# Four opening stages of a graph network kernel become one block

## The reference

```python
x_heads = jnp.einsum('ni,hij->nhj', x, W)          # node table: x @ W0
src = x_heads[row]; dst = x_heads[col]             # rows gathered by edge
edge_gate = jax.nn.sigmoid(edge_attr @ eg_w.T + eg_b)
e = einsum('ehd,hd->eh', src, a_src) + einsum('ehd,hd->eh', dst, a_dst) + edge_bias
```

## Time and profile before

| | |
|---|---|
| runs | 9183.11, 9192.17, 9197.33 us |
| median | 9192.17 us |
| span of the profiled execution | 9188.8 us (its own time outside the span is not recorded) |
| share of the span busy | PE 71%, DVE 69%, POOL 69%, ACT 18% |
| instructions | 193747 |

### The profile page before, as it was taken

One profiled execution on the slowest core, in us unless ns is written; L12 is line 12 of the kernel. 1 busy time (PEld: TensorE's weight loads), 2 busy tenths in 40 slices (PEclk: granted clock), 3 DMA queues, 4 the chain that ended last, 5 costly groups with the idle time before them and its releaser, 6 DMA issues. The chain is left out here.

```text
span 9188.8 us, 193747 instructions
## 1 busy us (share of the span) xinstructions
PE 6564.0 (71%) x41828; PEld 5489.2 (60%) x41829; DVE 6345.2 (69%) x11929; ACT 1632.9 (18%) x4649; POOL 6369.9 (69%) x7772
## 2 busy tenths in 40 slices
PE   5999999999378548777777625999768850037752
PEld 3878877888267536666666524777558740026652
DVE  3444444444577868777777524888768899999965
ACT  1111111110221134444444200111410000011100
POOL 2777777775068557777777764888367778877774
PEclk9999999999789879999999857999889975569975
DMA  3777777777067436666666769999359963359974
GB/s 115 207 206 208 208 207 206 209 207 200 24 177 210 128 113 211 209 208 209 209 209 208 213 172 157 273 270 270 103 163 264 259 188 86 87 159 256 253 210 115
DMA packets 2113959, 1742.97 MB, mean 190 GB/s; under 512 B 376688, under 2 KB 1838118, under 8 KB 2113686
## 3 DMA queue, kind: packets, MB, share of 16 engines
q1 hardware_dynamic: 1217548, 819.30, 30.4%
q10 hardware_dynamic: 710140, 472.87, 20.6%
q0 software_dynamic: 186160, 449.72, 17.3%
HBM read 1289.62 MB, written 453.29 MB: 190 GB/s over the span
## 5 line engine op out<-in xcount | busy, mean ns | idle before, releaser
L1592 POOL DMA_INDIRECT z_xg<-table,srci x1664 | 1819.1, 1093 | 512.9 <-issue 466.3
L1162 POOL DMA_INDIRECT sorted<-m_rows,srci x1612 | 1609.0, 998 | 532.4 <-issue 436.1
L464 POOL DMA_INDIRECT g_xg<-table,srci x1612 | 1582.1, 981 | 491.2 <-issue 464.3
L1458 PE MATMUL n_ps<-n_row,n_oh 128*128 128x257 f32 x3712 | 881.2, 389 | 216.0 <-DVE n_row L1434 198.1
L483 PE MATMUL g_psg<-g_wg,g_eT 128*128 128x136 f32 x3224 | 1027.6, 474 | 0.0
L1458 PEld LDWEIGHTS n_ps<-n_row,n_oh 128*128 128x128 f32 x3712 | 677.6, 190 | 419.5 <-issue 337.4
L500 PE MATMUL g_psx<-scores,g_hot 128*128 x3608 | 835.5, 362 | 70.3 <-DVE e_score L591 68.0
L483 PEld LDWEIGHTS g_psg<-g_wg,g_eT 128*128 128x128 f32 x3224 | 769.3, 324 | 191.0 <-issue 191.0
L500 PEld LDWEIGHTS g_psx<-scores,g_hot 128*128 128x128 f32 x3608 | 806.8, 329 | 86.9 <-issue 85.9
L1656 PE MATMUL z_ps<-z_wrow,z_oh 128*128 128x132 f32 x3712 | 603.4, 315 | 329.8 <-issue 188.8
L564 DVE TENSOR_TENSOR g_y<-g_gate,g_xg 128x512 f32<-128x512 f32 x403 | 279.7, 694 | 787.5 <-DMA g_xg<-table,srci 786.8
(11 more groups left out here) (411 smaller groups left out, 12549.7 us busy)
## 6 DMA issues: line engine op xcount, KB each, us to landing
n_row<-sorted SPq DMA_DIRECT2D x464, 520.0 KB, 4.4
z_buf<-gathered ACTq DMA_DIRECT2D x464, 256.0 KB
g_keys<-dst_row ACTq DMA_DIRECT2D x451, 256.0 KB
ag_buf<-gated SPq DMA_DIRECT2D x451, 256.0 KB, 3.2
m_keys<-dst_row ACTq DMA_DIRECT2D x451, 256.0 KB
gathered<-z_xg SPq DMA_DIRECT2D x416, 256.0 KB
gated<-g_y SPq DMA_DIRECT2D x403, 256.0 KB
g_eT<-in_attr_t SPq DMA_DIRECT2D x402, 256.0 KB
```

The lines of the kernel that those rows point to most:

```text
L464: nc.gpsimd.indirect_dma_start(out=xg[:, u, j, :], out_offset=None, in_=v.table[:, :], in_offset=bass.IndirectOffsetOnAxis(ap=v.srci[:, t: ...
L1162: nc.gpsimd.indirect_dma_start(out=v.sorted[:, :], out_offset=bass.IndirectOffsetOnAxis(ap=place[:, t:t + 1], axis=0), in_=rows[:, u, j, : ...
L1458: last = nc.tensor.matmul(ps[u % 4][:, 0:ROW], oh[:, u, j, :], row[:, u, j, 0:ROW], start=(j == 0), stop=(j == G - 1))
L1592: nc.gpsimd.indirect_dma_start(out=xg[:, u, j, :], out_offset=None, in_=v.table[:, :], in_offset=bass.IndirectOffsetOnAxis(ap=v.dsti[:, t: ...
```

## The change

One block, `stage_prologue`, takes the place of `stage_constants`, `stage_weights`, `stage_node_table` and `stage_steps` for the edges. In it:

- X is the first thing that SP loads, without a wait; its last part is cut into 96 and 10 nodes; `src_row` is gone; `dst_row` and the blanks come after the index tiles. Each group of loads has a semaphore of its own. `padrow` and `blank` are set by POOL.
- ACT loads the first layer's weights at once, with 8 DMAs of 32 words for its vectors where there were 16 of 16 words; the 14 loads of the other two layers' weights are issued by ACT after the first turn of the node table.
- The table is made in 25 pairs of blocks. PE transposes straight from X, ACT copies 256 columns, PE makes two products into one bank, and ACT copies 2 x 136 columns to `row` and 2 x 8 to `scores`. DVE has no part in it. The code is written out, with no loop. SP stores a pair at a time, 136 KB.
- DVE's chain for the steps runs beside it, and PE makes the two sums after pair 11.

`stage_clear` is gone: the gate stage sets only the last 52 x 8 words of each partition of `e_score`, on DVE ahead of its first wait. `stage_steps` keeps only what its other call needs (not shown). `v.after` and the DRAM tensor `src_row` are gone.

```diff
--- before.py
+++ after.py
@@ -59,98 +59,203 @@
-def stage_constants(nc, v):
...
+def stage_prologue(nc, v, steps, follows):
+    PAIRS, R = NBX // 2, 4
...
+            @block.sync
+            def _(sp):
+                sp.dma_start(v.X[:, 0:NB - 1, :], v.x[0:full, :].rearrange("(b p) c -> p b c", p=P)).then_inc(s_x, 16)
+                sp.wait_ge(s_set, 4)
+                sp.dma_start(v.X[0:cut, NB - 1, :], v.x[full:full + cut, :]).then_inc(s_x, 16)
+                sp.dma_start(v.X[cut:TAIL, NB - 1, :], v.x[full + cut:N, :]).then_inc(s_x, 16)
+                sp.dma_start(v.srci[:, 0:TE - 1], v.src_t).then_inc(s_src, 16)
+                sp.dma_start(v.srci[0:ETAIL, TE - 1:TE], v.src[(TE - 1) * P:E, None]).then_inc(s_src, 16)
+                sp.dma_start(dsti[:, 0:TE - 1], v.dst_t).then_inc(s_blk, 16)
+                sp.dma_start(dsti[0:ETAIL, TE - 1:TE], v.dst[(TE - 1) * P:E, None]).then_inc(s_blk, 16)
+                sp.wait_ge(s_pad, 2)
+                sp.dma_start(v.dst_row[:, 1:1 + E], v.dst[None, :]).then_inc(v.s_in, 16)
+                for place in (E + 1, E + 1 + half):
+                    sp.dma_start(v.dst_row[:, place:place + half], padrow[:, :]).then_inc(v.s_in, 16)
+                for line in (v.dst_row, v.sorted_row):
+                    sp.dma_start(line[:, 0:1], blank[:, 0:1]).then_inc(v.s_in, 16)
+                    sp.dma_start(line[:, TR * P + 1:TR * P + 2], blank[:, 0:1]).then_inc(v.s_in, 16)
+                for n in range(PAIRS):
+                    sp.wait_ge(s_row, n + 1)
+                    sp.dma_start(table[:, 2 * n:2 * n + 2, :], row[:, n % R, :, :]).then_inc(s_st[n % R], 16)
+                for u in range(R):
+                    sp.wait_ge(s_st[u], 16 * ((PAIRS - u + R - 1) // R))
+                sp.wait_ge(v.s_in, 16 * 7)
...
+                pe.wait_ge(s_w0, 16 * (2 + len(first.vectors)))
+                nc.tensor.matmul(ps_w[:, 0:2 * X8], first.wt[:, :], first.ab[:, :], start=True, stop=True).then_inc(s_ab, 1)
+                pe.wait_ge(s_x, 48)
+                pe.wait_ge(s_cp, 8)
+                def turn(n):
+                    if n >= 2:
+                        pe.wait_ge(s_xt, n - 1)
+                    for j in range(2):
+                        last = nc.tensor.transpose(ps_t[n % 2][:, j * P:(j + 1) * P], v.X[:, 2 * n + j, :], v.ident[:, :])
+                    last.then_inc(s_tr, 1)
+                def rows(n):
+                    if n == 0:
+                        pe.wait_ge(s_rhs, 1)
+                    if n >= 3:
+                        pe.wait_ge(s_row, n - 2)
+                        pe.wait_ge(s_sc, n - 2)
+                    pe.wait_ge(s_xt, n + 1)
+                    for j in range(2):
+                        last = nc.tensor.matmul(ps_r[n % 3][:, j * (W + X8):(j + 1) * (W + X8)], xt[:, n % 2, j * P:(j + 1) * P],
+                                                first.rhs[:, :], start=True, stop=True)
+                    last.then_inc(s_h, 1)
+                for n in range(PAIRS + 1):
+                    if n < PAIRS:
+                        turn(n)
+                    if n >= 1:
+                        rows(n - 1)
+                    if n == PAIRS // 2:
+                        pe.wait_ge(s_dve, 8)
+                        for d in range(2):
+                            last = nc.tensor.matmul(ps_s[d][:, :], v.ones[0:NBX, 0:P], started[0:NBX, d, :], start=True,
+                                                    stop=True)
+                        last.then_inc(s_pe, 1)
+                pe.wait_ge(v.s_w, 16 * sum(2 + len(w.vectors) for w in others))
+                for n, w in enumerate(others):
+                    nc.tensor.matmul(ps_w[:, (n + 1) * 2 * X8:(n + 2) * 2 * X8], w.wt[:, :], w.ab[:, :], start=True,
+                                     stop=True).then_inc(s_ab, 1)
+            @block.scalar
+            def _(act):
+                act.wait_ge(s_set, 1)
+                weight_loads(act, first, s_w0)
+                act.dma_start(first_i[0:NBX, :], v.dst_first.broadcast_to([NBX, GE])).then_inc(v.s_first, 16)
+                nc.scalar.preload_act_table(ACT.Copy)
+                def copy(n):
+                    if n >= 2:
+                        act.wait_ge(s_h, n - 1)
+                    act.wait_ge(s_tr, n + 1)
+                    nc.scalar.activation(xt[:, n % 2, :], ps_t[n % 2][:, 0:2 * P], ACT.Copy).then_inc(s_xt, 1)
+                def rows(n):
+                    if n >= R:
+                        act.wait_ge(s_st[n % R], 16 * (n // R))
+                    act.wait_ge(s_h, n + 1)
+                    made = ps_r[n % 3][:, 0:2 * (W + X8)].rearrange("p (t w) -> p t w", t=2)
+                    nc.scalar.activation(row[:, n % R, :, :], made[:, :, 0:W], ACT.Copy).then_inc(s_row, 1)
+                    nc.scalar.activation(v.scores[:, 2 * n:2 * n + 2, :], made[:, :, W:W + X8], ACT.Copy).then_inc(s_sc, 1)
+                for n in range(PAIRS + 1):
+                    if n < PAIRS:
+                        copy(n)
+                    if n >= 1:
+                        rows(n - 1)
+                    if n == 1:
+                        act.wait_ge(s_set, 6)
+                        for w in others:
+                            weight_loads(act, w, v.s_w)
...
+                nc.vector.memset(first.ab[:, :], 0.0).then_inc(s_set, 1)
+                nc.vector.memset(v.X[:, NB - 1:NBX, :], 0.0).then_inc(s_set, 1)
+                nc.vector.memset(v.srci[:, TE - 1:TR], PADKEY).then_inc(s_set, 1)
+                nc.vector.memset(dsti[:, TE - 1:TR], PADKEY).then_inc(s_set, 1)
+                for w in others:
+                    nc.vector.memset(w.ab[:, :], 0.0).then_inc(s_set, 1)
+                nc.vector.memset(v.ones[:, :], 1.0).then_inc(s_cp, 1)
+                nc.vector.memset(v.zeros[:, :], 0.0).then_inc(s_cp, 1)
...
+                dve.wait_ge(s_ab, 1)
+                nc.vector.tensor_copy(first.rhs[:, C:C + 2 * X8], ps_w[:, 0:2 * X8]).then_inc(s_rhs, 1)
+                link = chain(dve, s_dve)
+                dve.wait_ge(v.s_first, 16)
...
+                dve.wait_ge(s_src, 32)
+                nc.vector.tensor_copy(v.srck, v.srci[:, :]).then_inc(s_keys, 1)
+                dve.wait_ge(s_blk, 32)
+                nc.vector.tensor_copy(v.dstk, dsti[:, :]).then_inc(s_keys, 1)
+                dve.wait_ge(s_pe, 1)
...
+def weight_loads(queue, w, landed):
+    queue.dma_start(w.wt[:, :], w.wt_dram).then_inc(landed, 16)
+    queue.dma_start(w.rhs[:, 0:C], w.w_dram).then_inc(landed, 16)
+    for row, first, n, col in w.vectors:
+        queue.dma_start(w.ab[first:first + n, col], row, allow_slow_non_contiguous=True).then_inc(landed, 16)
...
-def stage_node_table(nc, v, name, rhs, table, scores, loads=(), kept=W):
...
@@ -529,6 +520,7 @@
             def _(dve):
+                nc.vector.memset(e_score[:, TE:TR, :], 0.0).then_inc(s_end, 1)
                 dve.wait_ge(s_w, 16 * (2 + 2 * H))
@@ -592,7 +584,7 @@
-                dve.wait_ge(s_end, 1)
+                dve.wait_ge(s_end, 2)
                 nc.vector.tensor_copy(hist[:, :], psc[:, 0:NBX]).then_inc(s_end, 1)
...
@@ -993,14 +985,6 @@
-def stage_clear(nc, v, name, x):
-    s = v.sem(name)
-    with nc.Block() as block:
-        @block.vector
-        def _(dve):
-            nc.vector.memset(x[:, :, :], 0.0).then_inc(s, 1)
@@ -2231,9 +2215,9 @@
-                ([(v.a0[h, 16 * s:16 * s + 16, :], 16 * h, 16, X8 * s + h) for h in range(8) for s in range(2)],
-                 [(v.a1[C:2 * C, :], 0, C, 0), (v.a1[0:C, :], 0, C, X8)],
-                 [(v.a3[h, 32 * (1 - s):32 * (1 - s) + 32, :], 32 * h, 32, 4 * s + h) for h in range(4) for s in range(2)]))):
+                ([(v.a0[h].rearrange("(s p) o -> p (s o)", s=2), 16 * h, 16, slice(h, None, X8)) for h in range(8)],
+                 [(v.a1[C:2 * C, :], 0, C, slice(0, 1)), (v.a1[0:C, :], 0, C, slice(X8, X8 + 1))],
+                 [(v.a3[h, 32 * (1 - s):32 * (1 - s) + 32, :], 32 * h, 32, slice(4 * s + h, 4 * s + h + 1)) for h in range(4) for s in range(2)]))):
...
-        v.src_row = dram("src_row", (1, TR * P), I32)
...
-            stage_constants(nc, v)
-        stage_weights(nc, v)
-        stage_node_table(nc, v, "t0", v.tables[0].rhs, v.table, v.scores)
-        stage_steps(nc, v, "se", None, GE, steps_e, follows)
+        stage_prologue(nc, v, steps_e, follows)
         start.close()
         with ExitStack() as layer:
             e_score = sb("e_score", [P, TR, X8], F32, layer)
-            stage_clear(nc, v, "ce", e_score)
             stage_gate(nc, v, e_score, gated, hist, steps_e)
```

More of the change, by code:

```diff
@@ L142, in _ @@
             @block.tensor
             def _(pe):
-                pe.wait_ge(v.s_w, 16 * sum(2 + len(w.vectors) for w in v.tables))
-                for n, w in enumerate(v.tables):
-                    last = nc.tensor.matmul(ps[:, n * 2 * X8:(n + 1) * 2 * X8], w.wt[:, :], w.ab[:, :], start=True, stop=True)
-                last.then_inc(s_p, 1)
```

(26 more changed lines are left out.)

243 lines of the change are left out of this document (60 added, 183 removed).

## The result

The changed kernel takes 9111.18 us (median of 9104.64, 9107.23, 9115.13 and 9123.81) beside 9192.66 (median of four: the three known ones and 9193.15). The ratio is 0.9913, 95% interval 0.9899 to 0.9927: 0.87% or 81 us less. The profiled execution is the one of 9104.64 us, span 9102.8, 86.0 under the 9188.8 of before.

What follows compares the result with a forecast made beforehand. A serial opening delays a gate paced by POOL. Gate start 26.7 + 5.8 + 17.1 + 2.5 + 3.5 = 55.6 us, 95.9 earlier than 151.46; 9192.2 − 95.9 = 9096.3 us, range 9060 to 9128.

Steps and rivals of the forecast that it cites:

- the likeliest case: The forecast itself: gate starts at 55.6 us, 95.9 earlier, giving 9096.3 us; chance 0.50.
- rival 1: Node-table pairs stay at the low clock, 1.46 us each: a gain of 83.9, 9108 us; chance 0.22.
- rival 2: Small weight loads in the opening are dear, 1.69 us each: gate at 75, 9116 us; chance 0.12.
- Start of the table: Opening: X issued at about 0.8 us in place of 10.24, first transpose at 16, open by −4 to +2.
- the bare store: X's last-part shape, stored at the kernel's end with nothing ahead of it, let go after 8.94 us.
- The hole: Opening, after the first pairs: ACT's 14 weight loads take 7.8 us, so pair 2's product starts at about 26.7.
- The pairs: Node table: 4 pairs at the low clock (5.8 us), then 19 at the high one (17.1 us).
- The sum over partitions: Opening: lies within PE's list now, taken as 2.5 us; 3.77 before at the low level.
- What was hidden: Opening: steps, block boundaries and the memset's 11.15 + 3.35 us leave the path; the gate's own memset, 0.35, is hidden.
- Whether time gained is kept: Gate: POOL paces it from its first gather, so an earlier start moves all behind it; 95.9 us kept.
- if any later stage changes its length: A condition under which the forecast would be wrong, for any stage behind the opening; no size given.
- The clock: Gate: PE is at the low level to the gate's end by durations, 434 ns a product, despite granted clock 1.00.

Runs made afterwards that it cites:

- e_pool: Changed kernel with the 14 loads of the other two layers' weights issued by POOL instead of ACT; gate starts at 46.4 us, ratio to the kernel before 0.9896.
- r_after: The changed kernel, unedited, profiled again on another chip: 10858.34 us, where the kernel before took 10969.55.
- e_memset: Kernel before with only the e_score memset moved into the gate and shrunk; 11058.01 us beside a median of 11053.27 for the kernel before.
- e_dve: Changed kernel with 61 idle one-word memsets on DVE at the end of the opening; 9109.27 us, aggregation 569.5.
- e_spcode: Changed kernel with 9 more instructions on SP in the opening, waits already met; 9097.58 us, aggregation 582.1.
- e_poolcode: Changed kernel with 11 idle one-word memsets on POOL in the opening; 9113.57 us, aggregation 581.7.
- e_hot: Changed kernel with 80 idle transposes on PE at the start of the gate; ratio to the kernel before 0.9905.

## Why the prediction held, point by point

The forecast was 9096.3 us, and 9111.18 was measured, inside the range of 9060 to 9128 and just above the likeliest case's own, 9086 to 9108. The total alone says little: 9108 and 9116, the times of rivals 1 and 2, lie nearer to it than the forecast's 9096.3. It is the rows of the opening that rule them out. The forecast came this close in part by luck, since errors of opposite sign partly cancel.

*Start of the table.* First transpose at 16, measured 16.10. The issue of X's last part took 9.79 us, near the 8.94 of the bare store and not the 13.26 of before.

*The hole.* 7.8 us for the 14 loads and the first product behind them at 26.7; measured 7.0 and 26.28. e_pool shows that it is on the path and worth 5.5.

*The pairs.* Here the gate's start was missed by 3.7 us, 55.6 against 51.9. The 23 pairs from 26.28 to the end of the last product at 49.05, less the sum's 1.98, took 20.8 and not 22.9, since two pairs ran low and not four and a pair at the high level takes 0.86 and not 0.90. The sum over partitions took 1.98 and not 2.5, the end 2.8 and not 3.5, and the hole's end was 0.4 earlier: 2.1 + 0.5 + 0.7 + 0.4 = 3.7. The mechanism was as put, though how many pairs run low is not fixed by the kernel (two here, three in r_after); rival 1, pairs at 1.46 throughout, is out, and so is rival 2: the loads took 0.5 us each on the mean.

*What was hidden.* The steps on DVE, the boundaries and the memset are gone from the path, as forecast: e_score's memset takes 0.41 us in the gate (0.35 forecast), beside the gate's own loads. e_memset gave this term alone, 14.8 measured and 14.50 by the rows.

*Whether time gained is kept.* "If its start moves, all behind it moves" is the step that failed. It holds for the gathers, 2074.8 and 2075.4 us. It doesn't hold for the aggregation, +12.6 us, which the experiments show to be a matter of the place of DVE's instructions: with the same early start and DVE's fill, e_dve has 569.5. The forecast named this kind of failure ("if any later stage changes its length") and gave it no price.

*The move stage.* +9.2 us is not settled. Its scatters took 1004 ns on the mean for 998. In e_spcode, which has the changed opening as well, they took 998 and the stage 2133.8, as in the kernel before; e_dve had 1002 and 2140.2, e_poolcode 1000 and 2137.8. So it moves by such amounts from one execution to another, and I take it for that, without having repeated the executions that would show its spread. Without it the changed kernel's profiled run would have ended near 9095.

*The sum of it.* The profiled span is 9102.8 for the 9092.9 forecast, 9.9 us longer: the opening is 3.7 shorter than forecast, the aggregation gives back 12.6, the move adds 9.2, and all other stages together are 8.4 shorter. The median is 8.4 above that span where the forecast added 3.4, which is 5.0 more. That makes the 14.9 us between 9096.3 and 9111.18.

*The clock.* That PE is at the low level through the gate, in spite of the column's 1.00, is borne out by the changed kernel. The same window of 1000 to 1400 us of it:

```profile
1000.00:1400.00 400.00, 387.33 (x1710) 319.93 (x1710) 195.77 (x544) 46.57 (x78) 305.19 (x312) 0.50 0.76 207
```

Same products, same busy time, and 0.50 in place of 1.00. The first change of level in the records of the kernel before is at 2386.5 us, and up to there the column shows full speed; after the change the first is at 29.2, and from then on the column agrees with the durations. So the mean clock of the kernel, 0.886 before and 0.76 after, fell without any product being slower.

## What to carry to other kernels

When a serial opening stands ahead of a stage that one engine's issues pace, price the opening by the time at which that stage starts, and expect to keep all of it there. Then compare the later loops one by one, by steps in a window of fixed length: an unrolled loop may run at another period because instructions were added to or taken from its engine's list far ahead of it, and most of a gain of 15 us can be lost in that, as e_memset shows. Test this with idle instructions on one engine at a time. And a hole in the path hides the next wait: with ACT's loads out of the way and PE at the high level, one wait for a store of the table took the next 1 us back.

## What the runs showed of the hardware

- The same loop of eight steps on DVE has two periods, 9.95 and 10.19 us, 2.3% of its stage, which go with the place of DVE's instructions: a few instructions fewer ahead of it are enough (830 for 832 in the compiled list). Data placed 512 bytes or 0.85 MB elsewhere made no difference, nor did other engines' instructions. What about the place matters, and how the gaps come about, stays open; only four places were tried, 832 and 840 with the short period, 779 and 830 with the long one.
- In e_hot TensorE ran the gate's first products at the high level (63.14 us) and was at the low one by 65.08. Its records followed each other without a pause in between, but it had been idle for 1.56 us just ahead of them, so whether the fall belongs to the gate's work or to that pause was not separated. In the kernel before and in the changed one it ran the whole gate, 2062 us, at 434 ns a product, the low level. The Trainium skill (TensorE: Matmul & The Clock Gate, Part 1, What's actually happening) says that activity releases the throttle. The pairs of the table, after two of them, agree with that; the gate doesn't. What the two differ in wasn't isolated.
- The granted clock of a stretch ahead of the first change of level in these traces reads 1.00 also where the products are at the low level (before, up to 2386.5 us; after, up to 29.2). A product of known shape tells the level: four fp32 records of 136 to 144 columns take 0.73 us or 1.17 to 1.33.
- Chips of one kind differ by a quarter and more in a stage with indirect gathers: 2075 to 2083 us up to the last of 1612 on two chips, 2630 to 2675 on three others, with 207 and 163 GB/s in the same window. The gather itself costs POOL the same (981 and 982 ns), and the aggregation, which moves 212 GB/s on the first chip (2600 to 3100 us) and 211 on the second (3200 to 3600), takes 569.4 us on both.
